# Attention sums: ten tiles folded by GpSimd, six by VectorE, and one set of narrow matmuls in place of two

## What is computed

```
q = (layernorm(x) @ Wq + bq)      # 4 x 1024 queries, 16 heads of 32
k, v = ctx @ Wk + bk, ctx @ Wv + bv    # 4 x 2048 keys
attn = softmax(clip(q k^T / sqrt(32), -1e4, 1e4))
x = x + tanh(g0) * ((attn @ v) @ Wo + bo)
x = x + tanh(g1) * ffn(layernorm(x))   # 512 -> 2048 -> 512, silu
```

## Time and profile before

| | |
|---|---|
| runs | 3056.42, 3062.79 and 3061.96 us, median 3061.96 |
| the profiled execution | 3066.97 us, its span 3065.2 us |
| PE busy | 2958.2 us, 97% of the span |
| DVE busy | 2152.3 us, 70% |
| ACT busy | 1632.5 us, 53% |
| POOL busy | 1834.8 us, 60% |
| granted TensorE clock, mean | 0.979 of full speed |
| attention loop | about from 460 to 2228 us of the span |

### The profile page before, as it was taken

How to read it: one execution, slowest core, us unless ns; L and a number is a source line. 1 busy time by engine, 2 the same in 40 slices (tenths; PEclk the granted TensorE clock), 3 DMA queues, 4 the chain that set the end, 5 groups by cost and what they waited for, 6 DMA issues and landing times. The chain is left out here.

```text
span 3065.2 us, 50985 instructions
## 1 busy us (share of the span) xinstructions
PE 2958.2 (97%) x14950; PEld 1792.3 (58%) x14950; DVE 2152.3 (70%) x3162; ACT 1632.5 (53%) x2967; POOL 1834.8 (60%) x882
## 2 busy tenths in 40 slices
PE   8999979999999999999999999999979799999999
PEld 6888754444444444444444444444437577777777
DVE  5555557777777777777777777777748787777775
ACT  3222226666666666666666666666631444444443
POOL 4655638888888888888888888888853000000000
PEclk9999979999999999999999999999989799999999
DMA  5666762222122222212222221222158200000000
GB/s 201 226 233 220 234 205 47 59 62 58 46 62 62 49 55 62 61 44 62 62 51 53 62 61 43 62 62 53 43 142 281 110 28 28 28 28 25 17 14 28
DMA packets 142418, 255.27 MB, mean 83 GB/s; under 512 B 18971, under 2 KB 61043, under 8 KB 135157
## 3 DMA queue, kind: packets, MB, share of 16 engines
q1 hardware_dynamic: 142324, 254.13, 29.3%
HBM read 162.32 MB, written 91.23 MB: 83 GB/s over the span
## 5 line engine op out<-in xcount | busy, mean ns | idle before, releaser
L947 DVE TENSOR_REDUCE at_half_max<-ps 128x1 f32<-128x1024 f32 x1024 | 1216.4, 1219 | 462.4 <-PE ps L740 456.7
L740 PE MATMUL ps<-k_stack,q_stack 96*128 96x512 f32 x2048 | 706.2, 427 | 16.9 <-issue 13.0
L759 PE MATMUL ps<-q_stack,k_stack 98*128 98x512 f32 x2048 | 657.0, 402 | 1.3 <-ACT probT L885 1.0
L885 ACT ACTIVATE probT<-ps 128x512 f32<-128x512 f32 x1024 | 536.2, 603 | 229.1 <-PE ps L759 229.0
L885 ACT ACTIVATE at_probT<-ps 128x512 f32<-128x512 f32 x1024 | 536.5, 603 | 220.2 <-PE ps L759 220.2
L740 PEld LDWEIGHTS ps<-k_stack,q_stack 96*128 96x128 f32 x2048 | 349.5, 191 | 494.9 <-issue 327.6
L605 POOL TENSOR_TENSOR at_gp_sum<-at_gp_sum,probT 128x1024 f32<-128x1024 f32 x256 | 610.2, 2384 | 21.4 <-ACT probT L885 0.4
L605 POOL TENSOR_TENSOR at_gp_sum<-at_gp_sum,at_probT 128x1024 f32<-128x1024 f32 x256 | 609.6, 2381 | 21.2
L759 PEld LDWEIGHTS ps<-q_stack,k_stack 98*128 98x128 f32 x2048 | 385.1, 188 | 173.7 <-ACT probT L885 53.0
L1497 POOL TENSOR_TENSOR x_keep<-x_keep,b_half 128x2048 f32<-128x2048 f32 x8 | 37.5, 4684 | 545.0 <-DVE x_keep L1520 545.0
L1550 DVE SCALAR_TENSOR_TENSOR ff_acc<-ps,s_t,ff_acc 128x512 f32<-128x512 f32 x384 | 288.0, 750 | 20.3 <-DVE ff_acc L1550 0.5
(11 more groups left out here) (199 smaller groups left out, 3877.4 us busy)
## 6 DMA issues: line engine op xcount, KB each, us to landing
k_stack<-kT_hi SPq DMA_DIRECT2D x128, 256.0 KB, 4.9
kT_hi<-pi_out_hi SPq DMA_DIRECT2D x16, 1024.0 KB, 4.4
kT_lo<-pi_out_lo SPq DMA_DIRECT2D x16, 1024.0 KB, 6.7
v_heads<-pi_v_out SPq DMA_DIRECT2D x16, 1024.0 KB, 10.5
q_stack<-qT_hi SPq DMA_DIRECT2D x128, 128.0 KB, 3.4
k_stack<-kT_lo SPq DMA_DIRECT2D x64, 256.0 KB, 4.3
v_head<-v_heads SPq DMA_DIRECT2D x64, 256.0 KB, 5.1
pi_c_in<-in_ctx_dram SPq DMA_DIRECT2D x16, 768.0 KB, 9.9
```

Of the source, the lines that this page charges most:

```text
L740: mm = pe.matmul(ps[:, n, :], q_stack[buf][0:PARTS, rows], k_stack[buf][0:PARTS, BANK * n:BANK * (n + 1)], start=True, stop=True)
L759: pe.matmul(ps[:, key_bank(lane, kv), :], k_stack[buf][0:rows, P * kv:P * (kv + 1)], q_stack[buf][0:rows, q:q + BANK], start=True, stop=Tr ...
L885: act.activation(probT[lane % 2][:, kv, :], src, ACT.Exp).then_inc(exp_done, 1)
L947: dve.tensor_reduce(dst, src, AX_X, ALU.max).then_inc(max_done, 1)
```

## The change

GpSimd's five additions now cover ten tiles: four of 128x1024 over tiles 0 to 9, and a fifth of 128x512 that adds the two halves, so that `gp_sum[:, 0]` is one tile. VectorE adds the other six tiles to two (`rest`, which lies in `clipped`) with two additions of 128x1024, `add_rest`, in the step at lag 12: the first behind the maximum of scores 0, 1, the second behind that of scores 2, 3. For the last two units (and if clipping) TensorE takes these six tiles itself. `last_sums` is gone: `fold_values` is one set with `partial`, `gp_sum[:, 0]` and the two tiles of `rest`, at lag 13, and stands at the end of the step, behind keys 2, 3. It waits for GpSimd's fifth addition and both of VectorE's. `gather` stays at lag 14 but comes first in the step, ahead of exponentials 0, 1. `copy_partial` waits for `fold_done` in place of `partial_read`.

```diff
+        rest = clipped[:, :].rearrange("p (a n) -> p a n", n=BANK)
+        def by_pe(unit, clipping):
+            return clipping or isinstance(unit, int) and unit >= UNITS - 2
...
-                for i in range(1, GP_ADDS):
+                for i in range(1, GP_ADDS - 1):
                     pool.wait_ge(exp_done, KVT * unit + 2 * i + 4)
                     pool.wait_ge(gp_added, GP_ADDS * unit + i)
                     pool.tensor_tensor(gp_sum[lane % 2][:, :, :], gp_sum[lane % 2][:, :, :],
                                        pairs[:, 2 * i + 2:2 * i + 4, :], ALU.add).then_inc(gp_added, 1)
+                pool.wait_ge(gp_added, GP_ADDS * unit + GP_ADDS - 1)
+                pool.tensor_tensor(gp_sum[lane % 2][:, 0, :], gp_sum[lane % 2][:, 0, :], gp_sum[lane % 2][:, 1, :], ALU.add) \
+                    .then_inc(gp_added, 1)
...
             def fold_values(base, slot):
...
                 pe.wait_ge(partial_done, unit + 1)
-                pe.matmul(ps[0:D, 7, :], A["fold"][:, :], partial[:, :], start=True, stop=True)
-                for g in range(1, 4):
-                    mm = pe.matmul(ps[D * g:D * (g + 1), 7, :], ones[:, :], probT[lane % 2][:, KVT - 5 + g, :],
-                                   start=True, stop=False)
-                mm.then_inc(partial_read, 1)
-
-            def last_sums(base, slot):
...
                 pe.wait_ge(gp_added, GP_ADDS * (unit + 1))
-                for g, tile in ((1, probT[lane % 2][:, KVT - 1, :]), (2, gp_sum[lane % 2][:, 0, :]),
-                                (3, gp_sum[lane % 2][:, 1, :])):
-                    mm = pe.matmul(ps[D * g:D * (g + 1), 7, :], ones[:, :], tile, start=False, stop=True)
+                pairs = probT[lane % 2]
+                tiles = [gp_sum[lane % 2][:, 0, :]]
+                if by_pe(unit, clipping):
+                    tiles += [pairs[:, kv, :] for kv in range(GP_TILES, KVT)]
+                else:
+                    pe.wait_ge(rest_added, 2 * (unit + 1))
+                    tiles += [rest[:, 0, :], rest[:, 1, :]]
+                mm = pe.matmul(ps[0:D, 7, :], A["fold"][:, :], partial[:, :], start=True, stop=True)
+                for i, tile in enumerate(tiles):
+                    g = i % 3 + 1
+                    mm = pe.matmul(ps[D * g:D * (g + 1), 7, :], ones[:, :], tile, start=(i < 3), stop=(i + 3 >= len(tiles)))
                 mm.then_inc(fold_done, 1)
...
-                fold_values(base, slot)
-                last_sums(base, slot)
                 scores(base, slot, 2)
                 scores(base, slot, 3)
                 keys(base, slot, 2)
                 keys(base, slot, 3)
                 project_at(base, slot, (2, 3))
+                fold_values(base, slot)
...
+            def add_rest(base, slot, i):
+                unit, lane, r = unit_at(base, slot, PV[1])
+                if unit is None or r or by_pe(unit, clipping):
+                    return
+                pairs = probT[lane % 2]
+                dve.wait_ge(exp_done, KVT * unit + KVT)
+                if i == 0:
+                    need(dve, fold_done, unit)
+                    dve.tensor_tensor(rest, pairs[:, GP_TILES:GP_TILES + 2, :], pairs[:, GP_TILES + 2:GP_TILES + 4, :],
+                                      ALU.add).then_inc(rest_added, 1)
+                else:
+                    dve.wait_ge(rest_added, 2 * unit + 1)
+                    dve.tensor_tensor(rest, rest, pairs[:, GP_TILES + 4:KVT, :], ALU.add).then_inc(rest_added, 1)
...
                     maxima(slot, s, 0)
+                add_rest(base, slot, 0)
                 shift(base, slot, 0)
                 shift(base, slot, 1)
                 if s is not None:
                     maxima(slot, s, 1)
+                add_rest(base, slot, 1)
                 split_maxima(base, slot)
```

More of the change, by code:

```diff
@@ L491, in attend @@
     KVT = SK // P
-    TURN, KEYS, PV, SUMS, FOLD = 7, 8, (11, 12), 13, 14
-    TAIL = FOLD + 1 - QT
+    TURN, KEYS, PV, FOLD, GATHER = 7, 8, (11, 12), 13, 14
+    TAIL = GATHER + 1 - QT
     RING = 3
@@ L496, in attend @@
     GP_ADDS = 5
+    GP_TILES = 10
     PARTS = 3 * D
@@ L549, in attend @@
         partial_done = sem("partial_done")
-        partial_read = sem("partial_read")
+        rest_added = sem("rest_added")
         fold_done = sem("fold_done")
@@ L798, in fold_values @@
             def fold_values(base, slot):
-                unit, lane, r = unit_at(base, slot, SUMS)
+                unit, lane, r = unit_at(base, slot, FOLD)
                 if unit is None or r:
@@ L803, in fold_values @@
                 pe.wait_ge(partial_done, unit + 1)
-                pe.matmul(ps[0:D, 7, :], A["fold"][:, :], partial[:, :], start=True, stop=True)
-                for g in range(1, 4):
-                    mm = pe.matmul(ps[D * g:D * (g + 1), 7, :], ones[:, :], probT[lane % 2][:, KVT - 5 + g, :],
-                                   start=True, stop=False)
-                mm.then_inc(partial_read, 1)
-            def last_sums(base, slot):
-                unit, lane, r = unit_at(base, slot, FOLD)
-                if unit is None or r:
-                    return
-                pe.wait_ge(gp_added, GP_ADDS * (unit + 1))
-                for g, tile in ((1, probT[lane % 2][:, KVT - 1, :]), (2, gp_sum[lane % 2][:, 0, :]),
-                                (3, gp_sum[lane % 2][:, 1, :])):
-                    mm = pe.matmul(ps[D * g:D * (g + 1), 7, :], ones[:, :], tile, start=False, stop=True)
+                pe.wait_ge(gp_added, GP_ADDS * (unit + 1))
+                pairs = probT[lane % 2]
[9 more added lines that the diff above has]
+                    mm = pe.matmul(ps[D * g:D * (g + 1), 7, :], ones[:, :], tile, start=(i < 3), stop=(i + 3 >= len(tiles)))
                 mm.then_inc(fold_done, 1)
@@ L899, in copy_partial @@
                 act.wait_ge(pv_done, unit + 1)
-                need(act, partial_read, unit)
+                need(act, fold_done, unit)
                 act.copy(partial[:, :], ps[:, 7, :]).then_inc(partial_done, 1)
             def gather(base, slot):
-                unit, lane, r = unit_at(base, slot, FOLD)
+                unit, lane, r = unit_at(base, slot, GATHER)
                 if unit is None or r:
@@ L907, in gather @@
                 act.wait_ge(fold_done, unit + 1)
-                heads_before = (BODY * base + (slot - FOLD) // QT) // HALVES if isinstance(base, int) else \
-                    BUFS * base + (slot - FOLD) // PER_HEAD
+                heads_before = (BODY * base + (slot - GATHER) // QT) // HALVES if isinstance(base, int) else \
+                    BUFS * base + (slot - GATHER) // PER_HEAD
                 need(act, stored[lane % 2], 64 * heads_before)
@@ L913, in step @@
             def step(base, slot):
+                gather(base, slot)
                 exps(base, slot, 0)
@@ L917, in step @@
                 copy_maxima(base, slot)
-                gather(base, slot)
                 exps(base, slot, 2)
@@ L1023, in step @@
                 shift(base, slot, 3)
-            run_steps(dve, step, STEPS, UNROLL, first=1, tail=TAIL if clipping else 0)
+            run_steps(dve, step, STEPS, UNROLL, first=1, tail=TAIL if clipping else PV[1] + 1 - 3 * QT)
         @block.vector
@@ L1041, in _ @@
             dve.wait_ge(max_done, 2 * STEPS)
+            dve.wait_ge(fold_done, UNITS - 2)
             for half in range(HALVES):
```

## The result

The changed kernel takes 3513.14 us in the median (3509.57 to 3517.58) against 3062.35 before: ratio 1.148 (95% interval 1.146 to 1.149), so 450.8 us slower. Its profiled execution has a span of 3509.3 us, 444.1 over the one of before. It lies in the attention loop: from the first `copy_partial` to the last it takes 2255.9 us where it took 1806.0, and all the rest is some 6 us shorter. VectorE adds in 126 of the units, so the whole is 444.1 / 126 = 3.52 us each.

What follows compares the result with a forecast made beforehand. TensorE was taken as the bound, busy 1766.6 of 1768 us. The profiled 3066.97 us plus 237 (blocked additions) plus 76 (clock) gave 3380, less 5 for the median 3375; likeliest case 3290 to 3460, whole range from 3160.

Steps and rivals of the forecast that it cites:

- Sign and mechanism: Attention loop: slower at 0.91, because a VectorE addition called during a GpSimd one waits for its end.
- The race: Second VectorE addition against GpSimd's first of the next unit: GpSimd starts first, by 0.17 us in the walked unit.
- the walk around the blocked addition: One attention unit: second VectorE addition takes 3.3 us (1215.71 to 1219.01), delaying fold and reductions; period 15.97 us.
- Blocked in every unit: Attention loop: the second VectorE addition waits in all 126 units, +1.88 us each, 237 us.
- The rival of alternation: Attention loop: VectorE wins the race in every other unit, mean 0.85 us, 3168 us, up to 3230; chance 0.11.
- the clock's term: TensorE in the attention loop: idle stretches drop the clock, 0.6 falls a unit at 1.0 us, 76 us.
- the twin: Two VectorE additions ending the attention stage before the change: one blocked, TensorE idle 1.40 us, then clock 2.4 to 1.2 GHz.
- The six stretches: Feed-forward stage, 10 us each with 1.0 to 3.3 us missing: clock below full after three; used for 0.6.
- The bound of 1.70: Upper price in us of one clock fall, from one value set's loss; 3513 if every unit; 0.08 above 3460.
- What the removed set is worth: One narrow TensorE set per unit: 1.22 us, period 12.87; only 0.19 arrives even if VectorE never waits.
- steps 12 to 14: Steps of an attention unit by lag: second value half, fold, last sums; VectorE claimed as the bound there.
- Small things: Last two units' three-round set, +1.0 us in all, and a drain 1.1 shorter: left at zero together.

Runs made afterwards that it cites:

- e8: Changed kernel with four needless wide matmuls per unit on TensorE ahead of the fold: 3310.40 us, ratio 1.081.
- e2: Changed kernel with GpSimd's five additions cut to 8 of 512 columns, result incomplete: 3054.83 us, ratio 0.998.
- e5: Changed kernel with both VectorE additions together behind the first reduction of the step at lag 12: 3322.47 us, ratio 1.085.
- e9: Changed kernel with two needless wide matmuls per unit on TensorE ahead of the fold: 3430.38 us, ratio 1.121.
- e10: Changed kernel with one needless wide matmul per unit on TensorE ahead of the fold: 3436.13 us, ratio 1.124.
- e4: Changed kernel without VectorE additions, TensorE summing the six tiles itself in every unit: 3158.13 us, ratio 1.031.
- e11: Changed kernel with GpSimd folding twelve tiles to two, no VectorE additions, TensorE summing six tiles in one group: 3052.00 us, ratio 0.997.
- e7: Changed kernel with the fold alone moved back between keys 1 and scores 2, 3: 3721.50 us, ratio 1.216.

## Why the prediction was wrong, point by point

- **Sign and mechanism: right.** 0.91 stood on slower. The race, the walk around the blocked addition and who is late behind it held to 0.1 us. Blocked in every unit, 1.88 x 126 = 237 us, measured 248 (e8). The idle stretch that the walk gave TensorE was too long, 2.3 against 1.92 us. The rival of alternation did not occur; e2 and e5 show that VectorE is undisturbed if GpSimd is away or later.
- **The step that failed is the clock's term**, "I take 0.6 falls a unit" at 1.0 us, 76 us. Measured 203 us (213 by the periods). One part of it is the number: the clock falls in every unit, not in six of ten, which alone makes 126 of the 76. I had counted idle stretches of the feed-forward stage and the twin together as if they were draws of one kind; e8 and e9 show a step between 1.0 and 1.4 us idle instead, and 1.9 lies beyond it (the twin fell at 1.40). The six stretches also left out one of that stage, from 2450 to 2470 us, after which the clock is below full. The other and larger part, from 126 to 203, is the price. A single fall is 1.0 us (e10) to 17.19 - 16.06 = 1.13: the estimate of 1.0 was right, and in e10 by the predicted way: both passes of the fold take 1.06 us instead of 0.62. In the units of 17.19 of the changed kernel the fold is over before the clock falls, and the pairs behind it pay. But in two of five units of the changed kernel the slow stretch is twice as long. In the unit of 18.77 the windows of TensorE alone read:

```profile
1087.00:1088.00 1.00, 1.00 (x3) 0.54 0.00 0
...
1090.00:1091.00 1.00, 1.00 (x4) 0.50 0.00 0
1091.00:1092.00 1.00, 1.00 (x4) 0.50 0.00 0
1092.00:1093.00 1.00, 1.00 (x5) 0.50 0.00 0
1093.00:1094.00 1.00, 1.00 (x12) 0.54 0.00 0
```

  It then reaches the value half, which takes 2.69 instead of 1.92. Together: 1.13 in every unit and about 1.4 more in two of five is 1.13 + 0.56 = 1.69, by 126 213 us, against 203 measured. Why some falls last twice as long was not settled; the rhythm of five units repeats through the whole stage, with one short unit more in two places, so it isn't noise.
- **The bound of 1.70 was in the text, and only as a price per fall** (3513 if in every unit): the range left it out with a chance of 0.08 on all that lies above 3460. The measured mean per unit, 203 / 126 = 1.61, is near that bound, and the time even meets its 3513, but that is luck: the 1.70 is what one value set lost, and no unit of the changed kernel pays it. They pay 1.13 or about 2.5. What the twin, the first fall of the trace inside this very loop, had right is that an idle stretch of this length is followed by a fall; I averaged that away with six rows of another stage.
- **What the removed set is worth: overstated, without effect on the sum.** The text first gave 1.22 us and then, in the walk, 0.19, and said that VectorE is the bound in steps 12 to 14. e2 has 14.07 instead of 13.9, so 0.02 to 0.05 us a unit (by period and by time) for the whole change with GpSimd away. e4 and e11 point at a reason for the rest, not tested singly: scores that had to wait for a bank are followed by their keys in 0.57, not 0.47 (1067.72 to 1068.29 in e4), and a step without narrow sets lasts 2.05 instead of 1.86.
- **Small things** at zero: not tested singly.

## What to carry to other kernels

Before giving VectorE an operation with two SBUF operands, look up in the timeline what GpSimd runs at the time of the call: if it has begun an addition, the price is the rest of that addition, for all that is queued behind. Then look at how long TensorE will stand for it: in this loop up to 1.0 us before the fold (1.48 in the whole unit) cost nothing beyond itself, and from 1.4 us (1.87) on nearly every unit paid another 1.0 us or more through the clock, so that filling it with needless matmuls gained 200 us. And take how often such a thing happens from a row of the same loop, even a single one, rather than from an average over other stages; its price depends on what stands where the slow stretch falls.

## What was unexpected of the hardware

- Needless matmuls made the kernel faster: four wide ones a unit, 3310 against 3513 us, because the granted clock stayed at 2.4 GHz in the loop.
- In this loop the step is narrow: 1.0 us idle before the fold (e8), no fall; 1.4 (e9), one in nearly every unit. It isn't the length of that one stretch alone, as 1.67 us in the kernel with both additions together left one unit in four without a fall.
- After 1.9 us idle the slow stretch was in two of five units twice as long as in the others, in an order of five units that repeats almost without exception. After 3.5 us idle (e7) units of a third, longer kind appear.
